# Half a shared matmul between two sums of the top-k search in an AdaLN mixture-of-experts kernel

## What is computed

```python
scores = jax.nn.softmax(xf @ gate_weight.T, axis=-1).T          # 8 x 4096
vals, idx = jax.lax.top_k(scores.reshape(-1), 2 * S)            # the 8192 best pairs of expert and token
gate = jnp.zeros((Ee, S), x.dtype).at[idx // S, idx % S].add(vals)
h = jax.nn.gelu(jnp.einsum('sd,edf->esf', xf, W1) + b1[:, None, :], approximate=True)
y = jnp.einsum('esf,efd->esd', h, W2) + b2[:, None, :]
out = jnp.einsum('es,esd->sd', gate, y)
shared = jax.nn.gelu(xf @ Ws1 + bs1, approximate=True) @ Ws2 + bs2
out = out + shared
```

## Time and profile before

| | kernel before |
|---|---|
| device time, median of 3 | 341.42 us (339.98 to 345.33) |
| span of the profiled execution | 356.2 us |
| PE busy | 277.9 us (78%), 1039 matmuls |
| POOL busy | 217.5 us (61%) |
| DVE busy | 151.9 us (43%) |
| ACT busy | 142.3 us (40%) |
| search, first to last sum on PE | 55.92 to 88.74 us |
| first gather on POOL | 99.57 us |
| first scatter on POOL | 162.28 us |
| mean granted TensorE clock | 0.915 |

### The profile page before, as it was taken

How to read it: one execution, slowest core, us unless ns; L and a number is a source line. 1 busy time by engine, 2 the same in 40 slices (tenths; PEclk the granted TensorE clock), 3 DMA queues, 4 the chain that set the end, 5 groups by cost and what they waited for, 6 DMA issues and landing times.

```text
span 356.2 us, 4620 instructions
## 1 busy us (share of the span) xinstructions
PE 277.9 (78%) x1039; PEld 142.0 (40%) x1039; DVE 151.9 (43%) x766; ACT 142.3 (40%) x237; POOL 217.5 (61%) x243
## 2 busy tenths in 40 slices
PE   5888878999987975859999999899939178697300
PEld 2666763443543443425454444344414033233100
DVE  2899845667775264624555543442211101101100
ACT  4759964444432322235444444355313023233100
POOL 4667840000065564636788788887887887788661
PEclk9999995999999889999999999999967869989855
DMA  7929310230045746534555455555554555343321
GB/s 206 271 90 265 93 30 0 59 45 2 0 143 140 229 115 169 138 92 81 111 116 112 74 97 103 110 115 114 116 114 88 80 106 123 76 59 53 33 25 14
DMA packets 49774, 35.70 MB, mean 100 GB/s; under 512 B 7816, under 2 KB 44495, under 8 KB 49744
## 3 DMA queue, kind: packets, MB, share of 16 engines
q0 software_dynamic: 13824, 14.46, 25.1%
q1 hardware_dynamic: 35794, 20.86, 20.4%
q10 hardware_dynamic: 126, 0.04, 0.0%
HBM read 23.40 MB, written 11.94 MB: 99 GB/s over the span
## 4 chain that ended last, share of the span: by engine, by line
POOL 33%; PE 20%; issue 19%; DVE 11%; DMA 6%; another core or an unknown queue 5%; ACT 2%; POOLq 1%; DVEq 1%; SPq 0%
POOL out_dram L986 27%; PE Y L1161 6%; PE U L1128 5%; POOL R L974 5%; DMA out_dram<-YO,IDXB 4%; DVE GJ L793 3%; PE Y L1059 2%; DVE HM L767 1%; PE LG L1080 1%; DVE ST L514 1%; PE R1b L1017 1%; PE R L1017 1%; ACT H2F L379 1%; POOLq L1000 1%
## 5 line engine op out<-in xcount | busy, mean ns | idle before, releaser
L986 POOL DMA_INDIRECT out_dram<-YO,IDXB x72 | 113.6, 1578 | 32.7 <-issue 20.1
L974 POOL DMA_INDIRECT R<-rows_scratch,IDXB x72 | 70.0, 972 | 81.9 <-DVE IDXB L808 60.2
L1134 PE MATMUL U<-XT,XW 128*128 128x512 f32 x144 | 78.3, 639 | 8.3 <-issue 6.0
L443 ACT ACTIVATE HF<-U,CB 128x512 f32<-128x512 f32 x72 | 49.4, 687 | 57.0 <-PE U L1134 39.8
L1161 PE MATMUL Y<-HF,XW 128*128 128x512 f32 x144 | 72.1, 596 | 0.0
L842 DVE SCALAR_TENSOR_TENSOR YO<-R1b,GT,R 128x128 f32<-128x128 f32 x72 | 20.3, 345 | 112.1 <-DMA out_dram<-YO,IDXB 51.6
L1134 PEld LDWEIGHTS U<-XT,XW 128*128 128x128 f32 x144 | 27.5, 205 | 39.1 <-issue 31.4
L443 ACT ACTIVATE HF<-U,COL 128x512 f32<-128x512 f32 x32 | 21.8, 686 | 47.6 <-PE U L1128 25.3
L1128 PE MATMUL U<-H2F,WS 128*128 128x512 f32 x64 | 37.8, 674 | 0.0
L1161 PE MATMUL Y<-HF,WS 128*128 128x512 f32 x64 | 36.8, 659 | 0.0
L1161 PEld LDWEIGHTS Y<-HF,XW 128*128 128x128 f32 x144 | 25.6, 190 | 23.4 <-issue 23.4
(11 more groups left out here) (178 smaller groups left out, 336.2 us busy)
## 6 DMA issues: line engine op xcount, KB each, us to landing
XW<-in_L_ffn_W_dram SPq DMA_DIRECT2D x36, 256.0 KB
XW<-in_L_attn_x_dram SPq DMA_DIRECT2D x8, 256.0 KB, 6.7
rows_scratch<-GBC SPq DMA_DIRECT2D x2, 1024.0 KB, 8.1
rows_scratch<-HT SPq DMA_DIRECT2D x8, 256.0 KB, 2.4
out_dram<-SHO SPq DMA_DIRECT2D x8, 256.0 KB
R<-rows_scratch,IDXB POOLq DMA_INDIRECT x72
out_dram<-YO,IDXB POOLq DMA_INDIRECT x72
INV<-in_inv_dram SPq DMA_DIRECT2D x3, 256.0 KB, 5.5
```

The source lines that it names most:

```text
L443: eng.activation(HF[:, g % RING, :], UB[g % 2][:, :], ACT.Gelu_apprx_tanh, bias=bias).then_inc(M["a_gelu"], 1)
L974: eng.indirect_dma_start(XG[:, v % XR, s, :], None, rows_dram, bass.IndirectOffsetOnAxis(ap=IDXB[:, v, s:s + 1], axis=0)).then_inc(M[f"ld_ ...
L986: eng.indirect_dma_start(out, bass.IndirectOffsetOnAxis(ap=IDXB[:, v, s:s + 1], axis=0), YO[:, v % 2, s, :], None, compute_op=ALU.add).the ...
L1134: eng.matmul(bank[:, :], WU[:, v % WR, c * P:(c + 1) * P], XT[:, v % 2, :], start=True, stop=True).then_inc(M["pe_up"], 1)
```

## The change

During the search (steps 0 to 15) a step now holds half an `up` and half a `down` (256 of the 512 columns) in place of whole ones, so that two steps make a chunk; `halves(s)` says which half. The first `down` of a block is not split: it stands whole in the even step. `up` and `down` count their semaphore up after the second half only. Chunks 10 to 31 follow whole in steps 16 to 37, where before chunks 16 to 31 stood in steps 16 to 31. UNIT1 becomes 16 + 32 - 10 = 38, so everything of the units comes six steps later, while the steps of the ties and lists stay. The last three closes move from steps 31, 33, 35 to 33, 37, 41.

```diff
-UNIT1 = GS0
+
+SEARCH = H0 // 2
+UNIT1 = SEARCH + GS0 - (2 + SEARCH // 2)
...
-CLOSE_AT = {21: 0, 23: 1, 25: 2, 27: 3, 29: 4, 31: 5, 33: 6, 35: 7}
+CLOSE_AT = {21: 0, 23: 1, 25: 2, 27: 3, 29: 4, 33: 5, 37: 6, 41: 7}
...
 def on_step(s):
 
-    if s < GS0:
-        return s if s >= 0 else None
+    if s < SEARCH:
+        return 2 + s // 2
+    if s < UNIT1:
+        return 2 + SEARCH // 2 + s - SEARCH
     v, c = unit_step(s)
     return GS0 + NC * v + c if c < NC and v < NU else None
+
+
+def done_on_step(s):
+
+    return on_step(s) - LAG if s < UNIT1 else on_step(s - LAG)
+
+
+def halves(s):
+
+    return (s % 2,) if s < SEARCH else (0, 1)
...
+                    lo, hi = parts[0] * BLK // 2, (parts[-1] + 1) * BLK // 2
+                    m = eng.matmul(bank[:, lo:hi], WS[:, c * P:(c + 1) * P], H2F[:, u * BLK + lo:u * BLK + hi],
+                                   start=True, stop=True)
+                    if 1 in parts:
+                        m.then_inc(M["pe_up"], 1)
                     return
...
-                if g is not None and g >= 2:
+                if g is not None:
                     with when(eng, g // NC - NB, used):
-                        up(g)
+                        up(g, halves(s))
                 half_step(2 * s)
-                g = on_step(s - LAG)
+                g = done_on_step(s)
                 if g is not None and g < GS0:
-                    down(g)
+                    if g % NC:
+                        down(g, halves(s))
+                    elif 0 in halves(s):
+                        down(g)
```

More of the change, by code:

```diff
@@ L469, in ye @@
                                    bias=CB2[:, v % 3, :]).then_inc(M["a_ye"], 1)
+            gelu(0)
+            gelu(1)
             for s in range(NSTEP):
@@ L475, in scalar @@
                 g = on_step(s)
-                if g is not None:
+                if g is not None and 1 in halves(s):
                     with when(eng, g // NC - NB, used):
@@ L480, in scalar @@
                     rows_out(ROWS_AT[s])
-                g = on_step(s - LAG)
-                if g is not None and g < GS0 and g % NC == NC - 1:
+                g = done_on_step(s)
+                if g is not None and g < GS0 and g % NC == NC - 1 and 1 in halves(s):
                     finish_shared(g // NC)
@@ L1116, in tensor, with up @@
                         turn_h2(j - 2)
-            def up(g):
+            def up(g, parts=(0, 1)):
                 u, c = g // NC, g % NC
@@ L1127, in up @@
                     eng.wait_ge(M["ld_ws"], 32)
-                    eng.matmul(bank[:, :], WS[:, c * P:(c + 1) * P], H2F[:, u * BLK:(u + 1) * BLK], start=True,
-                               stop=True).then_inc(M["pe_up"], 1)
+                    lo, hi = parts[0] * BLK // 2, (parts[-1] + 1) * BLK // 2
[3 more added lines that the diff above has]
+                        m.then_inc(M["pe_up"], 1)
                     return
@@ L1144, in tensor, with down @@
             turn_h2(NB - 3)
-            def down(g):
+            def down(g, parts=(0, 1)):
                 u, c = g // NC, g % NC
                 bank = YB[u % 2]
+                lo, hi = parts[0] * BLK // 2, (parts[-1] + 1) * BLK // 2
                 eng.wait_ge(M["a_gelu"], g + 1)
@@ L1160, in down @@
                         eng.wait_ge(M["a_ye"], u - 2 - NB + 1)
-                eng.matmul(bank[:, :], down_weights(g), HF[:, g % RING, :], start=c == 0,
-                           stop=c == NC - 1).then_inc(M["pe_dn"], 1)
+                m = eng.matmul(bank[:, lo:hi], down_weights(g), HF[:, g % RING, lo:hi], start=c == 0,
+                               stop=c == NC - 1 and hi == BLK)
+                if 1 in parts:
+                    m.then_inc(M["pe_dn"], 1)
             def bit(i):
```

## The result

| | before | changed |
|---|---|---|
| device time, median (lowest to highest) | 340.80 us (339.98 to 345.33, 4 runs) | 348.65 us (348.38 to 348.83, 4 runs) |
| span of the profiled execution | 356.2 us | 346.7 us |

The changed kernel takes 1.0215 times as long, with a 95% interval of 1.0171 to 1.0258: 2.2% slower. So a second profile of the kernel before, without them (e0_before_again, the first experiment), is the one to compare with.

What follows compares the result with a forecast made beforehand. Bound: POOL's DMA train behind the first scatter, held by PE's work between search and `yt(0)`. 10.3 us moved work, less 0.8 search gain and up to 4.1 hidden, gives 7.5: 341.42 + 7.5 = 348.9 us, range 343 to 353.

Steps and rivals of the forecast that it cites:

- A half costs half: PE in the search: a 256-column float32 matmul takes half a 512-column one, 0.43 us at 2.4 GHz, 0.86 at 1.2.
- Gaps of 0.97 us, a search of 28.7 us: Between sums: 22 of 29 gaps become DVE-bound at 0.97 us, first to last sum takes 28.7 us, not 32.82.
- the gaps with transposes: Two gaps of the search in which PE also does transposes: they stay near 1.04 us.
- The first sum 3.3 us late: Start of the search: three shared matmuls ahead of the first sum, at the lower clock, start it 3.3 us later.
- The search's gain: End of the search: with thinner gaps less the late first sum, the last sum comes 0.8 us earlier.
- The sign "last sum within 1.5 us of before": End of the search: if the forecast is right, the last sum starts within 1.5 us of its old start, 88.74.
- The moved work: PE between search and `yt(0)`: twelve matmuls add 10.3 us, 0 to 4.1 hidden in two waits; first scatter 7.5 us later.
- POOL passes it on one to one: Behind the first scatter: POOL's train of DMAs is unchanged and passes the 7.5 us shift on in full.
- POOL's wait ahead of the first scatter from 6.9 to about 15 us: Sign at POOL's first scatter: its wait for DVE's YO of unit 0 grows from 6.9 us to about 15.
- Rival 1: Ahead of the first scatter: gathers, not YO, release it, so the moved work is hidden; about 342 us, chance 0.20.
- Rival 2: Start of the search: first sum not held up, saving up to 4.7 us; with rival 1 336.7 us; chance 0.03.
- Rival 3: TensorE's clock falls or stays low in the search, all gaps 1.06 us; 351 to 356 us, chance 0.15.

Runs made afterwards that it cites:

- e0_before_again: The kernel before, unedited, profiled a second time without the four waits: 342.44 us, ratio 1.0021.
- e3: The changed kernel with halves only in the first 8 of the search's 16 steps, so two chunks move instead of six: 343.78 us, ratio 1.0077.
- e2: The changed kernel with 12 matmuls of chunks 25 to 31 cut to 4 of 512 columns: 347.76 us, ratio 1.0218.
- e11: The changed kernel, unedited, run again on a chip of the later runs: 351.07 us where before takes 341.58, ratio 1.0265.
- e9: The kernel before with 12 throwaway 512-column matmuls on PE behind list 8: 350.32 us where before takes 341.58, ratio 1.0289.
- e6: The kernel before with 12 throwaway 512-column matmuls behind list 8, on the chip with the four waits: 364.21 us where before takes 356.66, ratio 1.0223.
- e4: The changed kernel, unedited, on the chip with the four waits: 369.16 us where before takes 356.66, ratio 1.0373.
- e5: The changed kernel without shared matmuls ahead of the first sum, seven chunks moved, on the chip with the four waits: 366.40 us, ratio 1.0318.
- e7: The kernel before with three throwaway matmuls on PE ahead of the search, on the chip with the four waits: 355.33 us, ratio 0.9981.
- e8: The kernel before with three throwaway matmuls on PE ahead of the search, without the four waits: 340.96 us, ratio 0.9983.

## Why the prediction was right, point by point

*The time.* 348.9 us was forecast, 348.65 measured; slower by 2.2%, as forecast. Two terms of the sum were off, in opposite directions, and it was read from a disturbed execution; that it came within 0.3 us is in part luck.

*A half costs half.* Right: 0.43 us between starts at 2.4 GHz, and 0.86 at 1.2 GHz, from the start of the second half to that of the first sum (59.18 to 60.04 in e3, PE's timeline; e2 has 0.85). The first half takes 1.02 (59.31 less 58.29); why it takes 0.16 more is not shown.

*Gaps of 0.97 us, a search of 28.7 us.* Right: 0.96 us, and 28.22 and 28.27 us. That the gaps with transposes "stay" near 1.04 was misread: they are 1.42 us before and 1.00 in the changed kernel. The forecast did not use the 1.42, so the sum is not touched.

*The first sum 3.3 us late.* Right in its mechanism, and its size depends on when the clock rises. Less the 0.23 us that a first sum always needs, it is 3.3 us in e11 (clock up at 61.2), 3.5 in e2 and e3 (60.9 and 60.6), but 1.9 in the changed kernel's first profile, where the clock rose at 56.3, just as the first half began. The prediction took the lower level for all three matmuls, because it took 57 to 63 us of one execution as fixed. The Trainium skill, TensorE: Matmul & The Clock Gate, section "What's actually happening", says that the point at which the clock rises differs from run to run of the same kernel; these traces agree, with 56.3 and 61.2 us for the same program. The 500 ns that it gives for this are far less than the 4.9 us here. The search's gain, from the count on, is then 0.78 us in e11 (32.60 less 31.82; 0.8 forecast) and 2.27 us in the first profile (32.60 less 30.33). The sign "last sum within 1.5 us of before" did not come in the first profile: 86.34 is 2.4 us ahead of 88.74.

*The moved work.* 10.3 us was right as work (10.12 us more busy time). What was mis-sized is the part hidden: 0 to 4.1 us, with the middle taken. Undisturbed it is 0.96 us. The two waits of 2.33 and 1.80 us that were to be filled belong to the disturbed execution; in e0 PE has one of 0.73 and one of 0.94 us left there, of which the change keeps the first. So the handover grew by 9.08 us, not by 8.2 (10.3 less 2.05).

*What the prediction did not see.* Three things that stood ahead of list 8 in the kernel before, `xt(0)` and the first matmuls of unit 0 with their wait, stand behind it now. Last sum to list 8 is therefore 43.10 us in place of 45.22, and list 8 to `yt(0)` 20.15 in place of 8.87. Neither changes the sum, 9.16 us, and the gathers do not profit: POOL issues them without a pause, and the 36th comes 54.94 us after the last sum, 55.11 before.

*POOL passes it on one to one.* Nearly. The tail is 195.4 us in e0, 194.9 and 194.1 in the two profiles of the changed kernel, 194.2 in e9: where PE and POOL were just in step, up to 1.3 us comes back when the first scatter is later. In the forecast's own terms: 9.08 less 2.27, less 0.5 for the tail, is 6.3 us for the first profile; 9.08 less 0.78, less 1.3, is 7.0 us for e11. 7.5 was forecast, and the medians differ by 7.9 and by 9.5 us. The 1.5 to 2.5 us between are the size by which e0's profiled execution is slow: it took 344.27 us, 2.8 more than the median of 341.45 of the 25 executions beside it, while the changed kernel's two took 348.76 and 351.31, at their medians. Two things make it slow in the profile: the first count is ready at 57.81, 1.2 to 2.1 us later than in the profiles without a fall of the clock at 23 us, and the search starts at the lower clock. Beside an unedited search that starts at the upper clock (e6, 30.12 us from count to last sum) the changed kernel's 30.33 and 31.82 us gain nothing, and the same sums give 8.8 and 9.5 us (9.08 + 0.21 - 0.5; 9.08 + 1.70 - 1.3). So the search's gain, 0.8 us in the forecast, lies between 2.3 gained and 1.7 lost by the state of the clock in the two executions compared, and the whole between 6.3 and 9.5 us. Which of these is usual is not shown.

*POOL's wait ahead of the first scatter from 6.9 to about 15 us.* The growth was near (0.30 to 9.55), the two numbers themselves were wrong, since all of the 6.9 us but the 0.30 that POOL leaves between any two DMAs was the disturbance. (The 14.8 us that the prediction put between span and median compare a span with a time; between times it is some 17.) In e4, which has it, the wait is indeed 13.1 us.

*The rivals.* Rival 1, the moved work hidden, fell, though its condition half came: the gathers do stand on the chain in e0, but e0 shows POOL and YO in step, and e9 that ten microseconds more on PE arrive as ten. Rival 2's first half did happen in part (1.9 in place of 3.3 us) and was worth 1.5 us, too little to decide. Rival 3, a falling clock, was half right: it fell in the search for 3.4 us from 76.8 in the changed kernel's first profile, for 3.4 from 64.6 in e11 and for 6.9 from 77.1 in e4. It fell once in six of the seven profiles with halves through the whole search (not in e2), and in none of the six with whole matmuls, where PE is busy 31.59 of 32.37 us (e0), did it fall again once it was up. But it was back before the last sum each time, and its price was small: three gaps of 1.08, 1.07 and 1.00 us in place of 0.96, 0.27 us in all (0.31 in e11, 0.64 in e4). A gap costs 0.1 us more, as the rival had it, because half a matmul at 1.2 GHz still nearly fits into DVE's count; only three to six gaps paid it, not all 29.

## What to carry to other kernels

Thinning the work between two steps of a ring pays only as long as the thinned engine sets the step, here 4 of 32 us where the clock was low and 1.7 of 30 where it was not, while every matmul that is pushed behind the ring is paid in full if it lands in front of the next thing that another engine waits for: count the second before the first. Before the balance between two engines is read from a trace, compare that execution's time with the median of the runs; if it is far longer, the waits that look like slack may belong to that one execution. A matmul that stands ahead of a ring's first step costs whatever TensorE's clock is just then, which differs between executions of the same kernel.

## What the runs showed of the hardware

The four waits. In the first profile of before, DVE starts an instruction that needs PE's list sum several microseconds after that sum is done, and the profile names no engine of this core as releaser. DVE's timeline, 109 to 157 us:

```profile
109.58 0.16 DVE L783 TENSOR_TENSOR CNB<-PADM,R 128x3 f32<-128x3 f32 x1 [3.93 <-remote]
...
123.40 0.16 DVE L783 TENSOR_TENSOR CNB<-PADM,R 128x3 f32<-128x3 f32 x1 [4.68 <-remote]
...
137.16 0.16 DVE L783 TENSOR_TENSOR CNB<-PADM,R 128x3 f32<-128x3 f32 x1 [4.46 <-remote]
...
156.06 0.69 DVE L685 TENSOR_TENSOR SHO<-R1b,X 128x512 f32<-128x512 f32 x1 [5.64 <-remote]
```

PE had begun the sum that the first of them needs at 106.31 us and needed 0.28 us for it. ACT, which waits for other results of PE, starts again within 0.05 us of DVE at the first three:

```profile
109.62 0.69 ACT L443 ACTIVATE HF<-U,COL 128x512 f32<-128x512 f32 x1 [3.64 <-remote]
```

PE was busy for the whole of the first wait (3.93 of 3.93 us). So PE went on and both engines saw its results late. In e0 the same pair is 0.31 us apart (timeline of all engines):

```profile
108.00 0.28 PE L1230 MATMUL LG<-DQ,HM 128*128 128x129 f16 x2
108.31 0.16 DVE L783 TENSOR_TENSOR CNB<-PADM,R 128x3 f32<-128x3 f32 x1 [0.97 <-PE LG L1230]
```

The first three of before end 13.8 us apart. In the four profiles of the chip on which before takes 356.66 us (352.65 to 359.07) they are there too: at 107.00, 120.97 and 134.93 in e6, with the same spacing of 13.9 us, although the lists begin up to 2.2 us apart in these profiles. The 36th gather is issued between 154.4 and 154.7 us in all five of them, whatever stands ahead. This may be why e5 and e7 showed little there: a search that ends earlier is caught by the same wait. What holds the signal back was not found. The DMAs' share is high within the first three waits (0.68, 0.91 and 0.82, and 0.37 in the fourth), but e0 has 0.99 from 113 to 117 us and 1.01 from 117 to 121 without such a wait, so busy DMAs alone do not explain it. It stays open.

The front of the kernel varies too: in e0, e7 and e11 the clock fell once more at about 23 us for 3.4 us, and the first count is ready at 57.4 to 58.0 us; in the other eleven, without this fall, it is ready at 55.7 to 56.6. With a search of 29.9 or 32.4 us behind it, this could make some 4 of the 7 us between the lowest and the highest run of before beside e8 (338.5 to 345.4 us).
